# Attention, sampling and two recurrences on one core: q and k turned by transposing transfers instead of by TensorE, one-hot matrices by one comparison

## The chip, the cores and the metric

The kernel runs on one core of one Trainium2 chip. The metric is device time in microseconds of one execution, given as the median of several. Times inside an execution come from one profiled execution.

## The reference

The input x is (64, 64, 512), a condition is (64, 512). Four conditioned layers are each added to x:

```
x = x + attention(x, cond[:, None, :], W_emb, b_emb, g_norm, W_qkv, g_q, g_k, W_out)
x = x + sampling(x, cond)            # linear interpolation along the 64 tokens' features
x = x + gru_scan(cond, x, W_ih, W_hh, b_ih, b_hh)
x = x + rk4_scan(cond, cond, x, coupling, bias)
```

In attention, x is normalised by its root mean square, scaled and shifted by a modulation of the condition, and multiplied by W_qkv. Then, with 16 heads of 32:

```
q = _rms_norm(q, g_q)                # over the 32 features of a head
k = _rms_norm(k, g_k)
logits = jnp.einsum('bhqd,bhkd->bhqk', q, k) * d ** (-0.5)
attn = jax.nn.softmax(logits, axis=-1)
o = jnp.einsum('bhqk,bhkd->bhqd', attn, v)
return o + o @ W_out                 # after moving heads back
```

Sampling takes, for each batch row, the two features at floor and floor + 1 of a position given by the condition, and weighs them. The last two layers are scans over the 64 steps.

## The kernel before, in words

Two batch rows of 64 tokens make a pair of 128 tokens, which fill the partitions; there are 32 pairs, N0 being the last of them, N1 the one before. The first function, `attention_and_sampling`, works through 32 slots, one for each pair i; each engine has its own list of instructions for a slot, written out by hand, and waits on semaphores. In slot i TensorE projects pair i (`project`, three times 12 matmuls: q, k, v), computes the scores of pair i-1, mixes and projects out pair i-2, and samples pair i-3. All numbers of a matmul are f32 split into two f16 halves, high and low, and a product takes three matmuls (TERMS).

For q and k of a pair, in order: ScalarE squares the projections out of PSUM (`squares_qk`), VectorE sums them (`sums_qk`, `means`), ScalarE makes a guess of the reciprocal root by Ln and Exp (`guess`), VectorE corrects it (`newton`, three small instructions) and scales q and k by it (`scale_qk`) into the f32 tile qn. In the next slot TensorE turns qn (`turn_qk`, 8 transposes of 128x128 f32 into psA), ScalarE takes the high halves of what it turned (`high_qk`), with the gains g_q and g_k folded into q's by a scale for each partition, and VectorE the low halves (`low_qk`), both into qkT, which lies in the tile `first4` (`first` in the rows). Then `scores` runs. After scores, ScalarE computes exponentials (`exps`, 16 instructions of 128x64, one for each head, of which 2 stand ahead of the guess and 14 behind it), VectorE inverts the sums, GpSimd normalises (`norm_p`) and takes low halves (`low_halves`), and SP turns P's halves by two transposing transfers (`turn_p`, PT). The high half of V (`high_v`) stands on ScalarE behind the exponentials.

Sampling is a matmul with one-hot matrices E (in `room`). `load_rows` broadcasts the integer positions of one batch row to all partitions (`rows`, 128x512 f16), and `build` compares them with lidx, the index of a feature in its chunk, one comparison for each of 4 chunks. `weigh_taps` multiplies the samples by the interpolation weights, out of the PSUM banks that the projections of q and k use as well. So a projection waits for it:

```
            if n == 0:
                need(pe, qn_done, p.n * 2 - 1)
                need(pe, um_done, p.n * 2 - 7)
```

GpSimd modulates x of the next pair (`modulate`, two instructions), adds taps, and takes low halves of x. In slots 4 to 27 a piece of the recurrences' weights is loaded and split as well (`load_wr`, `high_wr`, `low_wr`). Before slot 0 come the condition's embedding (`high_we`, `low_we`, `embed`), the positions (`grid_front`, which waits for the condition, `condtok`), and the splitting of W_qkv. All loads but one stand in SP's queue.

The second function, `recurrences`, runs the 64 steps of both scans from about 610 us on; the change does not touch it.

## Time and profile before

| | |
|---|---|
| median of 3 runs | 1525.3 us (1524.68 to 1526.01) |
| profiled execution | 1528.0 us |
| its span | 1526.2 us |
| TensorE matmuls | 1472.8 us busy, 97% |
| VectorE | 1322.9 us, 87% |
| ScalarE | 902.6 us, 59% |
| GpSimd | 756.9 us, 50% |
| granted TensorE clock | 0.995 over the span |
| DMA | mean 55 GB/s; 100 to 130 GB/s up to about 600 us |

Busy time is the time in which an engine had an instruction at work. A busy TensorE in a stretch without idle brackets in its timeline sets the length of that stretch; another engine at a high share may still stand in a chain whose waits are what counts. In a timeline a bracket at the end of a row is the time in which the engine stood idle ahead of it and what ended that.

### The profile page before, as it was taken

How to read it: one execution, taken by the hardware profiler on the slowest of the kernel's cores; microseconds unless marked ns; L12 is line 12 of the kernel's file. 1: busy time of each engine (PE TensorE's matmuls, PEld its weight loads, DVE VectorE, ACT ScalarE, POOL GpSimd, SP SyncE). 2: the span in 40 equal slices, each digit the busy share in tenths (PEclk: the TensorE clock that was granted, in tenths of full speed). 3: DMA queues.
4: the chain of work that ended last, by engine and by line, in shares of the span. 5: the costliest groups of instructions: out<-in, count | busy, mean ns of one | idle time of the engine just before them, and what ended most of it. 6: DMA issues, size and time to landing. Idle time of an engine off the chain costs nothing.

```text
span 1526.2 us, 95000 instructions
## 1 busy us (share of the span) xinstructions
PE 1472.8 (97%) x42214; PEld 1308.4 (86%) x42214; DVE 1322.9 (87%) x3190; ACT 902.6 (59%) x2753; POOL 756.9 (50%) x916
## 2 busy tenths in 40 slices
PE   4799999999999999999999999999999999999997
PEld 2466677666776668999999999999999999999996
DVE  5888989988889878688888888888888888888887
ACT  5566776667766653555555555555555555555553
POOL 2567666666666754534434443443444344344432
PEclk9999999999999999999999999999999999999999
DMA  7255444545455432000000000000000000000000
GB/s 255 52 114 115 108 106 104 116 118 120 127 118 130 96 102 87 8 15 12 15 15 15 12 16 15 12 15 15 15 12 15 15 12 15 15 15 12 15 15 14
DMA packets 122602, 84.03 MB, mean 55 GB/s; under 512 B 68656, under 2 KB 107824, under 8 KB 122192
## 3 DMA queue, kind: packets, MB, share of 16 engines
q1 hardware_dynamic: 121968, 77.87, 20.3%
q8 instruction: 331, 5.42, 1.5%
q14 instruction: 79, 0.65, 0.2%
q10 hardware_dynamic: 224, 0.09, 0.0%
HBM read 42.23 MB, written 11.60 MB: 35 GB/s over the span
## 4 chain that ended last, share of the span: by engine, by line
PE 91%; DVE 4%; issue 2%; POOL 1%; ACT 1%; DMA 1%; SPq 0%; DVEq 0%; ACTq 0%; POOLq 0%
PE psB L1432 34%; PE psA L1461 15%; PE psQ L1146 15%; PE psA L1466 8%; PE psQ L1188 7%; PE psO L1234 5%; PE psO L1222 2%; PE psB L1170 2%; PE psA L1124 2%; DMA front<-in_cond 1%; POOL S L434 0%; DVE psO L1645 0%; POOL front L453 0%; DVE room L880 0%; PE psQ L1202 0%
## 5 line engine op out<-in xcount | busy, mean ns | idle before, releaser
L1432 PE MATMUL psB<-first,Wx 128*128 128x64 f16 x9216 | 290.3, 193 | 1.4 <-issue 1.1
L1432 PE MATMUL psB<-first,Whh 128*128 128x64 f16 x9072 | 287.0, 193 | 1.3 <-POOL first L1897 0.5
L1461 PE MATMUL psA<-ts,Cp 128*128 128x64 f16 x8160 | 280.7, 193 | 6.0 <-ACT ts L1532 6.0
L1432 PEld LDWEIGHTS psB<-first,Wx 128*128 128x128 f16 x9216 | 277.9, 98 | 2.0 <-issue 1.7
L1432 PEld LDWEIGHTS psB<-first,Whh 128*128 128x128 f16 x9072 | 274.1, 98 | 2.3 <-issue 1.4
L1146 PE MATMUL psQ<-Wx,front 128*128 128x512 f16 x1152 | 269.0, 384 | 4.1 <-DVE front L952 4.0
L1461 PEld LDWEIGHTS psA<-ts,Cp 128*128 128x128 f16 x8160 | 256.2, 98 | 7.0 <-ACT ts L1532 6.8
L1532 ACT ACTIVATE ts<-qst 128x256 f16<-128x256 f32 x192 | 80.1, 417 | 297.9 <-DVE qst L1645 297.9
L1146 PEld LDWEIGHTS psQ<-Wx,front 128*128 128x128 f16 x1152 | 108.9, 99 | 124.5 <-issue 5.0
L1897 POOL TENSOR_TENSOR en<-rz,dn 128x256 f32<-128x256 f32 x64 | 46.7, 730 | 259.8 <-issue 257.1
L1466 PE MATMUL psA<-ts,Cp 128*128 128x64 f16 x4080 | 161.2, 193 | 0.3 <-issue 0.3
L1672 DVE TENSOR_TENSOR ts<-psA,ts 128x256 f16<-128x256 f32 x255 | 107.3, 421 | 47.4 <-ACT psA L1532 47.4
L776 DVE TENSOR_SCALAR room<-rows,lidx 128x512 f16<-128x512 f16 x256 | 145.9, 612 | 0.3
L1466 PEld LDWEIGHTS psA<-ts,Cp 128*128 128x128 f16 x4080 | 136.9, 98 | 0.6 <-issue 0.4
L434 POOL TENSOR_TENSOR S<-S,rden 128x512 f32<-128x512 f32 x64 | 67.0, 1049 | 141.8 <-DVE rden L844 141.8
L518 ACT ACTIVATE S<-psB,mn 128x64 f32<-128x64 f32 x448 | 133.2, 338 | 0.0
L1645 DVE SCALAR_TENSOR_TENSOR rest<-cub,psQ 128x256 f32<-128x256 f32 x256 | 106.6, 416 | 7.3
L1645 DVE SCALAR_TENSOR_TENSOR psO<-qst,psO 128x256 f32<-128x256 f32 x253 | 107.2, 424 | 2.1
L1188 PE MATMUL psQ<-x,room 128*128 128x128 f16 x1856 | 108.5, 219 | 0.0
L1188 PEld LDWEIGHTS psQ<-x,room 128*128 128x128 f16 x1856 | 104.9, 98 | 0.1
L1897 POOL TENSOR_TENSOR V<-X3b,first 128x256 f32<-128x256 f32 x64 | 46.9, 733 | 115.9 <-DVE first L1759 114.6
L518 ACT ACTIVATION_READ_ACCUMULATOR S<-psB,mn 128x1 f32 x448 | 104.2, 233 | 0.0
(194 smaller groups left out, 2890.4 us busy)
## 6 DMA issues: line engine op xcount, KB each, us to landing
front<-in_x SPq DMA_DIRECT2D x32, 256.0 KB, 3.1
XR<-in_x_turned SPq DMA_DIRECT2D x32, 256.0 KB, 3.4
rows<-rows_dram SPq DMA_DIRECT2D x64, 128.0 KB, 3.0
out<-ob SPq DMA_DIRECT2D x63, 128.0 KB, 1.7
x<-x SPq DMA_DIRECT2D x29, 224.0 KB
Whh<-in_W_qkv SPq DMA_DIRECT2D x12, 256.0 KB, 8.4
room<-in_W_hh SPq DMA_DIRECT2D x12, 256.0 KB, 2.7
room<-in_W_ih SPq DMA_DIRECT2D x12, 256.0 KB, 3.0
```

The costliest lines, as they stand in the source:

```text
L518: return nc.scalar.activation(out, in_, f, **k)
L776: e = v.tensor_scalar(E_of(p, b)[:, k, :], rows[b][:, :], lidx[:, k:k + 1], None, ALU.is_equal)
L1146: last = mm(psQ[:, n, :], xn[p.u][:, i, c, :], Wqkv[:, j, c, n * D:(n + 1) * D], start=(c == 0 and t == 0), stop=(c == KC - 1 and t == 2))
L1188: last = mm(o[:, m, :, :], E_of(p, b)[:, c, m * PART:(m + 1) * PART], x1_of(p)[:, :, i, c, b, :], start=(c == 0 and i == 0), stop=(c == KC ...
L1234: last = mm(psO[:, m, :], Wo[:, i, c, m * PART:(m + 1) * PART], oT[:, j, c, :], start=(c == 0 and t == 0), stop=(c == KC - 1 and t == 2))
L1432: last = mm(o, W_[:, i, c, g * PART:(g + 1) * PART], src[:, j, c, :], start=False, stop=False, skip_group_check=True)
L1461: mm(psF[:, s % 2, m, :], Cp[:, i, c, m * PART:(m + 1) * PART], ts_[:, 0, c, :], start=(c == 0 and m == 0 and i == 0), stop=False, skip_gr ...
L1466: last = mm(psF[:, s % 2, m, :], Cp[:, 0, c, m * PART:(m + 1) * PART], ts_[:, 1, c, :], start=False, stop=(c == KC - 1), skip_group_check= ...
L1532: return nc.scalar.activation(out, in_, f, **k)
L1645: return v.scalar_tensor_tensor(out=flat(out), in0=flat(in0), scalar=scalar, in1=flat(in1), op0=ALU.mult, op1=op1)
L1672: v.tensor_tensor(ts_[:, 1, :, :], th, ts_[:, 0, :, :], ALU.subtract).then_inc(S["ts_ready"], 1)
L1897: return nc.gpsimd.tensor_tensor(flat(out), flat(in0), flat(in1), op)
```

## The change

For all pairs but the last, q and k are scaled into PSUM (psA), q is multiplied there by a row of gains, and both are split into f16 halves in the layout in which tokens are partitions; the halves (`qkh`, in the tile qn) are turned into qkT by two transposing transfers on SP's queue in the pair's own slot. TensorE turns only the last pair. `exps` is split into 2, 6 and 8, with the high halves of q and k between the six and the eight. The positions are stored four times, with 0, 128, 256 and 384 taken off, so that `rows` is 128x2048 and `build` is one comparison. The gains are loaded by broadcast (128x1024 f32) on ScalarE's queue, and so is the condition, which left SP's queue.

```
...
+        def turn_qk(p, n):
+            sp.wait_ge(qk_low, p.n * 2 + n + 1)
+            need(sp, sc_done, p.n)
+            sp.dma_start_transpose(qkT[:, n, :, :, :].rearrange("p i c n -> p (i c) n"), qkh[:, n, :, :].rearrange("p i n -> p (i n)"))\
+                .then_inc(qk_in, 16)
...
+            if i < NP - 1:
+                turn_qk(pair(0), 0)
+                turn_qk(pair(0), 1)
             if p := pair(-2):
                 load_rows(p, 1)
...
-                sp.dma_start(condtok, cond).then_inc(cond_in, 16)
...
         act.dma_start(vT[:, :], vectors).then_inc(vectors_in, 16)
+        act.dma_start(gains2.rearrange("p v n -> p (v n)"), gains.rearrange("v n -> (v n)").partition_broadcast(PART)).then_inc(vectors_in, 16)
+        act.dma_start(condtok, cond).then_inc(vectors_in, 16)
...
         def high_qk(p, n):
+            act.wait_ge(qn_done if n else q_gained, p.n * 2 + 2 if n else p.n + 1)
+            need(act, qk_in, p.n * 32)
+            a(qkh[:, n, 0, :], psA[:, n, :]).then_inc(qk_hi, 1)
...
-            if p := pair(-1):
-                if p.n > 1:
-                    exps(p, 2, HEADS)
-                    high_halves(p, 0)
-                else:
-                    exps_at_once(p)
+            p = pair(-1)
+            if p and p.n > 1:
+                exps(p, 2, HEADS // 2)
+            high_qk(pair(0), 0)
+            high_qk(pair(0), 1)
+            if p and p.n > 1:
+                exps(p, HEADS // 2, HEADS)
+                high_halves(p, 0)
+            elif p:
+                exps_at_once(p)
...
         def low_qk(p, n):
             dve.wait_ge(qk_hi, p.n * 2 + n + 1)
+            v.tensor_tensor(qkh[:, n, 1, :], psA[:, n, :], qkh[:, n, 0, :], ALU.subtract).then_inc(qk_low, 1)
...
-            for k in chunks:
-                e = v.tensor_scalar(E_of(p, b)[:, k, :], rows[b][:, :], lidx[:, k:k + 1], None, ALU.is_equal)
-            if chunks[-1] == KC - 1:
-                e.then_inc(e_built, 1)
+            v.tensor_scalar(E_of(p, b).rearrange("p c n -> p (c n)"), rows[b][:, :, :].rearrange("p c n -> p (c n)"),
+                            lidx[:, 0:1], None, ALU.is_equal).then_inc(e_built, 1)
...
         def scale_qk(p):
             dve.wait_ge(rs_step, (p.n + 3) * STEPS)
-            need(dve, qk_T, p.n)
+            to = sq if p.n == NP - 1 else psA
...
+                if n == 0 and p.n < NP - 1:
+                    dve.wait_ge(qn_done, p.n * 2 + 1)
+                    v.tensor_tensor(psA[:, 0, :], psA[:, 0, :], gain_row[:, :], ALU.mult).then_inc(q_gained, 1)
...
         def scores(p):
-            pe.wait_ge(qk_ready, p.n + 1)
+            if p.n == NP - 1:
+                pe.wait_ge(qk_ready, 1)
+            else:
+                pe.wait_ge(qk_in, 32 * (p.n + 1))
...
         def slot(pair, i):
-            if p := pair(-1):
-                turn_qk(p)
             project(pair(0), 0)
```

Where instructions stand now shows best in one steady slot. VectorE before, from the means of pair i on to the scaling of x for a later pair (ms are the means, rt and rs the Newton step, room the one-hot matrix, um the weighed samples, Whh a piece of weights):

```order
L785 TENSOR_SCALAR ms<-ss 128x33
L776 TENSOR_SCALAR room<-rows,lidx 128x512 x2
L865 TENSOR_TENSOR oT<-psO,oT 128x512
L790 TENSOR_TENSOR rt<-rs 128x33
L792 SCALAR_TENSOR_TENSOR rt<-rt,ms 128x33
L794 SCALAR_TENSOR_TENSOR rs<-rt,rs 128x33
L805 TENSOR_TENSOR qn<-psQ,rs 128x512 x2
L844 RECIPROCAL rden<-den 128x8
L776 TENSOR_SCALAR room<-rows,lidx 128x512 x2
...
L870 SCALAR_TENSOR_TENSOR XR<-psO,XR 128x4x128
L811 TENSOR_TENSOR Vt<-psQ,Vt 128x512
L847 TENSOR_TENSOR um<-psQ,WT 128x512
```

VectorE in the changed kernel, the same stretch:

```order
L804 TENSOR_SCALAR ms<-ss 128x33
L887 TENSOR_TENSOR oT<-psO,oT 128x512
L809 TENSOR_TENSOR rt<-rs 128x33
...
L813 SCALAR_TENSOR_TENSOR rs<-rt,rs 128x33
L824 TENSOR_TENSOR psA<-psQ,rs 128x512
L829 TENSOR_TENSOR psA<-psA,gain_row 128x512
L824 TENSOR_TENSOR psA<-psQ,rs 128x512
...
L796 TENSOR_SCALAR room<-rows,lidx 128x2048
L766 TENSOR_TENSOR qn<-psA,qn 128x512 x2
...
L892 SCALAR_TENSOR_TENSOR XR<-psO,XR 128x4x128
L833 TENSOR_TENSOR Vt<-psQ,Vt 128x512
L869 TENSOR_TENSOR um<-psQ,WT 128x512
```

Two comparisons left the place ahead of the Newton step, a multiplication by the gains stands between the two scalings, and the low halves of q and k (L766) stand ahead of V's low half, not in the next slot.

ScalarE before, from the squares of k on (front<-psQ; S are the exponentials, Vt the high half of V):

```order
L518 ACTIVATE front<-psQ 128x512
L518 ACTIVATE S,den<-psB,mn 128x64 x2
L518 ACTIVATE oT<-psO 128x512
L518 ACTIVATE lm<-ms 128x33
L518 ACTIVATE rs<-lm 128x33
L518 ACTIVATE S,den<-psB,mn 128x64 x14
L518 ACTIVATE front<-S 128x512
L518 ACTIVATE Vt<-psQ 128x512
```

ScalarE in the changed kernel:

```order
L530 ACTIVATE front<-psQ 128x512
L530 ACTIVATE S,den<-psB,mn 128x64 x2
L530 ACTIVATE oT<-psO 128x512
L530 ACTIVATE lm<-ms 128x33
L530 ACTIVATE rs<-lm 128x33
L530 ACTIVATE S,den<-psB,mn 128x64 x6
L530 ACTIVATE qn<-psA 128x512 x2
L530 ACTIVATE S,den<-psB,mn 128x64 x8
L530 ACTIVATE front<-S 128x512
L530 ACTIVATE Vt<-psQ 128x512
```

The high halves of q and k (qn<-psA) moved from the head of the next slot into the middle of the fourteen exponentials, ahead of V's.

## Rows read from the trace of the kernel before

**Rows 1.** The page, busy times and one costly group (busy, mean ns, idle):

```profile
PE 1472.8 (97%) x42214; PEld 1308.4 (86%) x42214; DVE 1322.9 (87%) x3190; ACT 902.6 (59%) x2753; POOL 756.9 (50%) x916
...
L776 DVE TENSOR_SCALAR room<-rows,lidx 128x512 f16<-128x512 f16 x256 | 145.9, 612 | 0.3
```

**Rows 2.** Timeline of TensorE in one slot: start us, us, instruction

```profile
283.52 1.04 PE L1124 MATMUL psA<-ident,qn 128*128 128x128 f32 x8
284.39 2.75 PE L1146 MATMUL psQ<-Wx,front 128*128 128x512 f16 x12
287.08 1.13 PE L1170 MATMUL psB<-first 32*64 32x64 f16 x96
...
290.83 1.20 PE L1222 MATMUL psO<-PT,Vt 64*32 64x64 f16 x96
```

**Rows 3.** Timeline of TensorE, the turns 27 slots apart

```profile
92.66 1.04 PE L1124 MATMUL psA<-ident,qn 128*128 128x128 f32 x8
...
561.02 1.04 PE L1124 MATMUL psA<-ident,qn 128*128 128x128 f32 x8
```

**Rows 4.** Timeline of ScalarE in the same slot

```profile
290.94 0.60 ACT L518 ACTIVATE front<-psQ 128x512 f32<-128x512 f32 x1 [2.12 <-PE psQ L1146]
...
293.23 0.23 ACT L518 ACTIVATE rs<-lm 128x33 f32<-128x33 f32 x1
293.36 0.30 ACT L518 ACTIVATE S<-psB,mn 128x64 f32<-128x64 f32 x1
...
297.42 0.71 ACT L518 ACTIVATE front<-S 128x512 f16<-128x512 f32 x1
297.94 0.67 ACT L518 ACTIVATE Vt<-psQ 128x512 f16<-128x512 f32 x1
```

**Rows 5.** Timeline of VectorE in the same slot

```profile
284.63 0.67 DVE L760 TENSOR_TENSOR front<-XR,psB 128x512 f32<-128x512 f32 x1
...
291.57 0.69 DVE L798 TENSOR_REDUCE ss<-front 128x16 f32<-128x512 f32 x1 [0.56 <-ACT front L518]
292.36 0.57 DVE L785 TENSOR_SCALAR ms<-ss 128x33 f32<-128x33 f32 x1
...
293.97 0.18 DVE L790 TENSOR_TENSOR rt<-rs 128x33 f32<-128x33 f32 x1
...
294.64 1.29 DVE L805 TENSOR_TENSOR qn<-psQ,rs 128x512 f32<-128x512 f32 x2
...
298.64 0.69 DVE L811 TENSOR_TENSOR Vt<-psQ,Vt 128x512 f16<-128x512 f32 x1 [0.25 <-ACT Vt L518]
299.25 0.68 DVE L847 TENSOR_TENSOR um<-psQ,WT 128x512 f32<-128x512 f32 x1
```

**Rows 6.** Line 315, P's transposing transfers: issue ns min/median/max, landing

```profile
L315 SPq DMA_TRANSPOSE PT<-front x60: 1231/1284/2365, 57.6 to 561.4; - x60
...
DMA to landing us min/median/max: 3.0/3.2/5.2
```

**Rows 7.** DMA issues: count, KB each, median us to landing

```profile
rows<-rows_dram SPq DMA_DIRECT2D x64, 128.0 KB, 3.0
...
Cp<-in_W_emb SPq DMA_DIRECT2D x2, 512.0 KB, 4.6
```

**Rows 8.** The chain that ended last, and ScalarE's timeline, at the start

```profile
4.53 8.27 DMA front<-in_cond
...
13.26 0.63 ACT L518 ACTIVATE Wx<-Whh 128x512 f16<-128x512 f32 x1 [2.00 <-DMA Whh<-in_W_qkv]
18.98 0.20 ACT L518 ACTIVATE lm<-ms 128x1 f32<-128x1 f32 x1 [5.08 <-DVE ms L785]
```

**Rows 9.** Timeline of TensorE, scores of pair 0

```profile
43.42 0.97 PE L1170 MATMUL psB<-first 32*64 32x64 f16 x96 [0.89 <-DVE first L754]
```

**Rows 10.** Timeline of GpSimd in the steady slot, its last before a pause

```profile
291.73 1.15 POOL L460 TENSOR_TENSOR front<-front 128x512 f16<-128x512 f32 x1
```

**Rows 11.** Timeline of VectorE, a Newton step beside GpSimd's work

```profile
36.31 0.34 DVE L790 TENSOR_TENSOR rt<-rs 128x33 f32<-128x33 f32 x1 [1.56 <-ACT rs L518]
```

More of the change, by code:

```diff
@@ L60, in need, with program @@
     eng.wait_ge(sem, value)
-def program(nc, x, x_turned, cond, cond_turned, vectors, W_emb, W_qkv, W_out, W_ih, W_hh, coupling_turned, out, rows_dram, wih_dram):
+def program(nc, x, x_turned, cond, cond_turned, vectors, gains, W_emb, W_qkv, W_out, W_ih, W_hh, coupling_turned, out, rows_dram, wih_dram):
     B, T, D = x.shape
@@ L160, in attention_and_sampling @@
     x1 = sb("x1", [PART, 2, 2, KC, 2, T], F16)
-    rows = [sb(f"rows{u}", [PART, D], F16) for u in range(2)]
+    rows = [sb(f"rows{u}", [PART, KC, D], F16) for u in range(2)]
     um = [sb(f"um{u}", [PART, KC, 2, T]) for u in range(2)]
@@ L917, in grid_rows @@
             dve.wait_ge(grid_step, 8)
-            v.tensor_copy(i0h, i0).then_inc(rows_ready, 1)
+            for c in range(KC):
+                last = v.tensor_scalar(i0h[:, c, :], i0, 1.0, float(-c * PART), ALU.mult, ALU.add)
+            last.then_inc(rows_ready, 1)
         def grid_weight():
@@ L976, in slot @@
                 grid_middle()
-            if tap and tap.n > 0:
-                build(tap, 0, (0,))
-            if p := pair(-1):
-                low_qk(p, 0)
-                low_qk(p, 1)
             if tap:
-                build(tap, 0, (1, 2, 3) if tap.n > 0 else range(KC))
+                build(tap, 0)
             if i == 1:
@@ L1999 @@
         vectors=np.concatenate(vectors, axis=0).T,
+        gains=np.stack([np.tile(inputs[n], D // inputs[n].shape[0]) for n in ("L0_cond_g_q", "L0_cond_g_k")]),
         W_emb=inputs["L0_cond_W_emb"], W_qkv=inputs["L0_cond_W_qkv"], W_out=inputs["L0_cond_W_out"],
```

121 lines of the change are left out of this document (59 added, 62 removed).

## The prediction

> **What bounds the kernel now.** I read first the page's busy times: TensorE works 1472.8 us of the span [rows 1], so it is the bound on average, but an average does not say where. The timeline of TensorE in one steady slot [rows 2] says it for the attention stage, which is all that the change touches: the turn of q and k (8 transposes, L1124) starts at 283.52, the first projection at 284.39, scores at 287.08, the second projection ends and mixing starts at 290.83, with no bracket of idle time anywhere. From turn to turn, over 27 slots, it is (561.02 - 92.66) / 27 = 17.35 us [rows 3], so the next turn is due at 283.52 + 17.35 = 300.87 and the next projection at 301.74. The turn takes 284.39 - 283.52 = 0.87 us of it. So TensorE is full, and an edit that takes work from it gains what the next-longest cycle allows. That cycle runs through ScalarE and VectorE, and I followed it in their timelines [rows 4, 5]: from the end of the second projection at 290.83 to the end of the first weighing of taps, 299.25 + 0.69 = 299.94, which is what the next slot's first projection waits for (`um_done`, same PSUM bank). Before, that is 1.8 us before that projection: slack.
>
> **What is taken away.** 31 of the 32 turns by TensorE go: 31 x 0.87 = 27 us of TensorE. If nothing else held it, a slot would be 17.35 - 0.87 = 16.48 us.
>
> **What is added on the cycle.** I walk the slot of [rows 2, 4, 5] with the new order of instructions.
> 1. Squares end at 290.94 + 0.60 = 291.54, the sums at 291.57 + 0.69 = 292.26, the means at 292.36 + 0.57 = 292.93, the Exp of the guess at 293.23 + 0.23 = 293.46. Unchanged.
> 2. VectorE's Newton step started at 293.97, behind two comparisons; they are gone from there, so it can start at 293.49 and ends 0.67 later (293.97 to 294.64, where the scaling starts) at 294.16.
> 3. Scaling of q 0.69 (two take 1.29, one 0.04 more than half), 294.85. Then the new multiplication by the gains, PSUM to PSUM, 128x512 f32. No row shows it; the nearest are the scalings at 0.65 each [rows 5]. Bounds: 0.65 and, if a PSUM destination costs as much again, 1.29. I take 0.69 and its hop: 295.57. Scaling of k starts one pitch (0.61) after the gain's start and ends at 296.17.
> 4. ScalarE meanwhile has done six of the fourteen exponentials: 14 take 297.42 - 293.36 = 4.06, 0.29 each, so it is free at 293.36 + 1.74 = 295.10 and waits for q until 295.60. The high halves of q and k cost like the squares out of PSUM, 0.60, with a pitch of 0.50: k's starts when its scaling is done, 296.20, and the remaining eight exponentials start at 296.70 and are over at 299.02. Before, all fourteen were over at 297.42: 1.60 later.
> 5. High half of P 0.52 (297.42 to 297.94), high half of V 0.67: 300.21. Low half of V starts behind it (before: 298.64, 0.03 behind), weighing one pitch of 0.61 later (298.64 to 299.25) and 0.69 long: 301.54. TensorE's projection can start at about 301.57.
>
> So from the end of the second projection to the next first projection it is 301.57 - 290.83 = 10.74 us, and from there over the first projection and scores to the end of the second is 290.83 - 284.39 = 6.44: a cycle of 17.18 us. TensorE itself would be ready after 16.48, so it now stands for 0.70 us in front of the first projection of each slot. **The gain is 17.35 - 17.18 = 0.17 us a slot, x 27 = 4.6 us**, not 0.87 x 27 = 23.5.
>
> **What lies beside it.** The low halves of q and k on VectorE fall into its wait for the exponentials; the one comparison over 128x2048 in front of them replaces four of 128x512, which are on no path that I found. No row shows it: it costs something above nothing and at most what four do, 4 x 0.612 = 2.4 us [rows 1]; I take 0.7. The turn itself is now a transfer: low half of k ready at 296.3 + 0.7 + 2 x 0.65 = 298.3 (1.7 later at the dear end), two issues of 1.28 each, the second from about 299.1, landing 3.2 behind its issue [rows 6]: 302.3. Scores come 2.70 after the projection's start, at 304.26: hidden by 1.9 us, by 0.2 at the dear end of the comparison. If that cover goes, each us late is a us of slot. On SP's queue behind them stand the load of the second row of indices (now 512 KB instead of 128 KB) and P's two transposing transfers. The 128 KB load lands in 3.0, a 512 KB one in 4.6 [rows 7], so I price the larger one at +1.6 us; it is wanted a slot later. P's transfers are issued about 2 us later than before, because P is, and would land about 1 us before mixing wants them.
>
> Here a rule of the Trainium skill bears on the transfer. DMA: Bandwidth & Descriptors, Latency and other measured facts, gives a transposing transfer an effective 261 GB/s; by it 256 KB is an estimated 1.0 us of transport, and the two would still be hidden. The rows show 3.2 from issue to landing and decide.
>
> **The start.** The longest single piece of the chain at the beginning is the load of the condition, issued at 4.53 and 8.27 long, and VectorE's low halves of W_emb queue behind what waits for it, so that the first guess (ScalarE, 18.98) waits 5.08 us [rows 8]. The change issues this load early from ScalarE's queue. The guess is then held by the first piece of W_qkv, whose load ScalarE waited for until 13.26 [rows 8]. The new 512 KB of gains goes in front of it, about 2 us, so 15.3, and the activation (0.63): 15.9 to 16.1 instead of 18.98. I take 2.7 us off the start; bounds 0 (the gains cost what the condition gave) and 5.
>
> **The first slots and the end.** In slots 1 and 2 the exponentials come behind the high halves of q and k, and pair 0's scores, at 43.42 before [rows 9], now wait for transfers that I place at 45.3: 1.9 later; the 0.87 no longer spent at the next turn gives part back. I take +1 us, bounds -1 and +3. At the end the turn of the last pair but one is gone as well: -0.9.
>
> **Sum.** -4.6 - 2.7 + 1.0 - 0.9 = -7.2 us against the profiled execution's own 1528.0 (span 1526.2 and 1.8 around it), which is 2.7 above the median of the runs shown: 1520.8 there, **1518 us** as a median.
>
> **The rivals.**
> - *TensorE stays the bound.* If the cycle is 0.7 us shorter than I worked out (the exponentials or halves overlap better), a slot is 16.5: -0.87 x 27 = -23.5, with the rest -26: 1499 to 1502. For it speaks that every added duration is a neighbour's; against it that the order of ScalarE's queue forces 1.6 us in. Chance 0.15.
> - *GpSimd gets in the way (ends slower).* VectorE's multiplication by 1/rms for the next pair, after which GpSimd starts, ended at 284.63 + 0.67 = 285.30, 5.5 us ahead of 290.83; now it stands behind the later weighing and ends about 4.6 ahead of it, and 3.8 where a weight's low half comes between. GpSimd's last work before its pause ended at 291.73 + 1.15 = 292.88 [rows 10]; it would end at 293.8 to 294.6, across the Newton step (293.49 on). When the two ran together at the start, the first instruction of that step took 0.34 [rows 11] against 0.18 [rows 5], so the step 1.2 against 0.67; the means would stretch too. With 0.47 more the cycle is 17.65, 0.30 longer than before: +8.1, with the rest +5.5: 1531. It decides from 0.17 on, where the gain per slot is gone. Chance 0.24.
> - *Late transfers.* If the q/k or P transfers queue behind the 512 KB loads, with landings like the longest seen, 5.2 [rows 6], scores or mixing wait. At 0.5 us a slot over mine it is +9, with the rest about 1531 to 1534. For it: two more transposing transfers and 768 KB more a slot; against: 1.9 us of cover. Chance 0.09.
> - *It cancels* within the start and slots: 1523 to 1528. Chance 0.12.
>
> On the second, the Trainium skill, GPSIMD Engine Reference, Specifications, says that GpSimd shares its SBUF interfaces with VectorE, with contention for instructions with two SBUF inputs or in a two-port mode. By that rule, the trace agrees: 0.34 against 0.18.
>
> **Numbers.** My forecast has 0.40, its own range 1511 to 1524 (cycle 16.95 to 17.35). The range over all, 1500 to 1533, leaves out part of the first and of the third rival and the far end of the second. Faster by over 0.2% (3 us, about what a measurement of this kernel can tell from no change): 0.40 + 0.15, and a little of the others: 0.58. Within: 0.15. Slower: 0.27.
>
> **What would show it.** Right: slots of 17.2 us, a bracket of about 0.7 us in front of L1162's first projection released by VectorE's weighing; ScalarE's fourteen exponentials split six and eight with k's half at about 5.4 us after the second projection; transposing q/k transfers landing over 1 us before scores; the first guess near 16.2 instead of 18.98. Wrong: no idle time before the projection (first rival); Newton instructions at 0.3 us or more (second); brackets in front of scores or mixing released by a DMA (third).

## The result and the profile after

The changed kernel takes **1547.1 us** (median of 4 runs, 1545.2 to 1548.7) against 1525.7 us of the kernel before on the same chip: a ratio of 1.0138, 95% interval 1.0121 to 1.0154. It is 1.4% slower; I had forecast it 0.5% faster. The profiled execution has a span of 1543.3 us, 17.1 more than that of before; the medians lie 21.4 apart, and the profiles locate the 17.1. One of the eight executions of e11 (below) took 3677 us, like no other, and its ratio leaves it out.

The first question is in which stage. The view by windows gives both kernels, cut at the same events (first projection, projection of slot 4, projection of slot 31, start of the recurrences); columns are the stretch and its length, busy time of the five engines with instruction counts, granted clock, DMA share, GB/s. The kernel before:

```profile
0.00:24.51 24.51, 5.81 (x98) 5.37 (x98) 11.82 (x24) 11.68 (x20) 0.86 (x9) 0.98 0.92 294
24.51:93.53 69.02, 55.90 (x825) 32.63 (x826) 56.84 (x100) 39.15 (x103) 37.84 (x36) 0.93 0.40 95
93.53:561.90 468.37, 464.17 (x9424) 333.10 (x9422) 418.19 (x758) 317.54 (x1264) 319.24 (x325) 1.00 0.48 111
561.90:612.30 50.40, 45.70 (x1200) 38.92 (x1198) 39.30 (x78) 18.20 (x32) 22.76 (x33) 1.00 0.38 110
612.30:1526.20 913.90, 901.23 (x30672) 898.44 (x30672) 796.80 (x2235) 516.02 (x1335) 376.21 (x514) 1.00 0.05 14
```

The changed kernel:

```profile
0.00:20.97 20.97, 5.43 (x97) 4.75 (x98) 12.41 (x25) 11.89 (x20) 0.86 (x9) 0.93 0.95 320
20.97:96.50 75.53, 58.22 (x794) 30.84 (x795) 60.30 (x100) 41.33 (x107) 39.23 (x36) 0.84 0.58 141
96.50:578.70 482.20, 448.07 (x9209) 310.84 (x9207) 352.90 (x624) 319.31 (x1262) 341.68 (x325) 1.00 0.77 181
578.70:627.70 49.00, 45.29 (x1198) 38.71 (x1199) 31.84 (x52) 16.91 (x30) 26.35 (x35) 1.00 0.60 177
627.70:1543.30 915.60, 900.84 (x30672) 897.38 (x30672) 796.60 (x2235) 515.89 (x1335) 376.23 (x514) 1.00 0.05 14
```

| stage | before | after | difference |
|---|---|---|---|
| to the first projection | 24.5 | 21.0 | -3.5 |
| slots 0 to 3 | 69.0 | 75.5 | +6.5 |
| 27 slots | 468.4 (17.35 each) | 482.2 (17.86 each) | +13.8 |
| end of the attention | 50.4 | 49.0 | -1.4 |
| recurrences (not touched) | 913.9 | 915.6 | +1.7 |

The page answers to [rows 1] and [rows 7] with TensorE's busy time and the rows' load:

```profile
PE 1457.9 (94%) x41966; PEld 1282.5 (83%) x41966; DVE 1254.1 (81%) x3033; ACT 905.3 (59%) x2753; POOL 784.3 (51%) x916
...
rows<-rows_dram SPq DMA_DIRECT2D x64, 512.0 KB, 5.2
```

In the 27 slots TensorE has 16 us less to do (464.2 to 448.1), so it works 99% of the time before and 93% after: it no longer sets the length of a slot. The DMA share goes from 0.48 to 0.77, which no line of the prediction looked at as a whole.

What TensorE waits for is in the view of waits of the changed kernel, 90 to 560 us (engine, what is held <- by what: us in total, times, longest; PEld is the weight load, PE the matmul behind it, so the two see the same wait and are not to be added):

```profile
PEld psQ L1162 <- issue: 24.4, 31, 1.3
PEld psO L1241 <- DMA PT<-front: 18.9, 17, 2.3
PE psQ L1162 <- DVE um L869: 18.3, 24, 1.1
PE psO L1241 <- DMA PT<-front: 10.6, 11, 1.8
```

Two waits share the slot. ("Issue" is time for which the profile shows no releaser; most of it on the first projection's weight load stands beside the matmul's wait for L869.) The first projection waits for the weighing of taps (L869) in 24 of 27 slots, as forecast; the weight loads of mixing (L1241) wait for P's transposing transfers in 17 slots and its matmuls in 11, which was forecast not to happen. One slot of the changed kernel, its timelines, start and length. TensorE, with the first projections of two slots:

```profile
293.68 2.75 PE L1162 MATMUL psQ<-Wx,front 128*128 128x512 f16 x12 [0.43 <-DVE um L869]
...
299.96 1.20 PE L1241 MATMUL psO<-PT,Vt 64*32 64x64 f16 x96
...
311.36 2.75 PE L1162 MATMUL psQ<-Wx,front 128*128 128x512 f16 x12 [1.14 <-DVE um L869]
```

VectorE:

```profile
301.49 0.76 DVE L804 TENSOR_SCALAR ms<-ss 128x33 f32<-128x33 f32 x1
...
302.81 0.56 DVE L809 TENSOR_TENSOR rt<-rs 128x33 f32<-128x33 f32 x1
...
304.60 0.70 DVE L829 TENSOR_TENSOR psA<-psA,gain_row 128x512 f32<-128x512 f32 x1
...
305.91 0.70 DVE L796 TENSOR_SCALAR room<-rows,lidx 128x2048 f16<-128x2048 f16 x1
```

GpSimd and ScalarE:

```profile
301.05 1.16 POOL L459 TENSOR_TENSOR x<-XR,x 128x512 f16<-128x512 f32 x1
302.16 1.16 POOL L472 TENSOR_TENSOR front<-front 128x512 f16<-128x512 f32 x1
305.33 1.19 ACT L530 ACTIVATE qn<-psA 128x512 f16<-128x512 f32 x2 [0.79 <-DVE psA L829]
```

SyncE's DMA queue:

```profile
307.24 2.64 SPq L325 DMA_TRANSPOSE first<-qn x2
309.93 0.57 SPq L291 DMA_DIRECT2D rows<-rows_dram x1
311.39 2.80 SPq L319 DMA_TRANSPOSE PT<-front x2
```

Read them against [rows 2, 4, 5]. From the start of mixing (299.96; 290.83 before) to the first projection it is 11.40 us, forecast 10.74. The new operations cost what was assumed: multiplication by the gains 0.70 (assumed 0.69), comparison over 128x2048 0.70 (0.7). But GpSimd's last two subtractions now end at 303.32, across the means and the Newton step, and these take 0.76 and 0.56 where [rows 5] have 0.57 and 0.18, together 0.57 of the 0.66 us (the rest is mostly a longer hop from the weighing to the projection). No wait for P's transfers stands in this slot, and it lasts 311.36 - 293.68 = 17.68 us.

How they are stretched can be read from the ends. GpSimd's subtractions end at 302.21 and 303.32, the means at 302.25 and the first Newton instruction at 303.37. The same holds throughout: between 90 and 560 us every one of the 26 means and of the 18 Newton instructions that took over 0.25 us ends 0.03 to 0.06 us behind the end of a GpSimd instruction. So they were held until it was over, not slowed by a factor. The kernel before has this too: all 26 of its long means end in that way, the 0.57 of [rows 5] among them (292.93, behind 292.88 of [rows 10]).

On SyncE's queue the second rows' load goes out 1.5 us ahead of P's transfers; before it went out 2.8 us ahead, with a quarter of the bytes. Line 319 (P), landing behind issue, minimum, median and maximum; [rows 6] had 3.0/3.2/5.2:

```profile
DMA to landing us min/median/max: 3.1/4.7/6.4
```

### The profile page after: what moved, and what is told of

Read it like the earlier page. It is cut to its first block, busy times and chain, and to the rows that moved or that the text cites. A ratio compares the mean times of both kernels' runs of the same rounds, so it can differ in the third digit from the quotient of the medians.

```text
span 1543.3 us, 94377 instructions
## 1 busy us (share of the span) xinstructions
PE 1457.9 (94%) x41966; PEld 1282.5 (83%) x41966; DVE 1254.1 (81%) x3033; ACT 905.3 (59%) x2753; POOL 784.3 (51%) x916
## 4 chain that ended last, share of the span: by engine, by line
PE 68%; DVE 11%; ACT 7%; DMA 5%; issue 5%; POOL 4%; SPq 0%; DVEq 0%; ACTq 0%; POOLq 0%
PE psB L1448 34%; PE psA L1477 15%; PE psA L1482 7%; PE psQ L1162 7%; DMA PT<-front 4%; ACT S L530 4%; DVE psA L824 3%; POOL front L452 2%; ACT front L530 1%; PE psB L1189 1%; DVE oT L887 1%; POOL S L446 1%; PE psQ L1207 1%; PE psO L1241 1%; PE psO L1253 1%
## 5 line engine op out<-in xcount | busy, mean ns | idle before, releaser
L1162 PE MATMUL psQ<-Wx,front 128*128 128x512 f16 x1152 | 275.7, 392 | 24.4 <-DVE um L869 19.7
L446 POOL TENSOR_TENSOR S<-S,rden 128x512 f32<-128x512 f32 x64 | 78.1, 1223 | 160.6 <-DVE rden L866 160.6
L817 DVE TENSOR_REDUCE ss<-front 128x16 f32<-128x512 f32 x64 | 43.8, 685 | 86.3 <-ACT front L530 86.3
L530 ACT ACTIVATE front<-psQ 128x512 f32<-128x512 f32 x64 | 38.1, 596 | 119.7 <-PE psQ L1162 119.7
```

The lines of the kernel that those rows point to most:

```text
L446: nc.gpsimd.tensor_tensor(part, part, rden[:, 8 * h:8 * h + 8].unsqueeze(2).broadcast_to([PART, HEADS // 2, T]), ALU.mult)\
L530: return nc.scalar.activation(out, in_, f, **k)
L1162: last = mm(psQ[:, n, :], xn[p.u][:, i, c, :], Wqkv[:, j, c, n * D:(n + 1) * D], start=(c == 0 and t == 0), stop=(c == KC - 1 and t == 2))
```

## The experiments

Ratios are to the kernel before on the same chip, in brackets the 95% interval. The runs were on several chips, on which the kernel before took 1523.8 to 1529.1 us (medians), so two runs are compared by their ratios: 0.001 is 1.5 us. For the steady slots I read the distance of the first and last of 27 turns of rs (one a slot, 26 distances): 17.86 us in the changed kernel, 17.35 before. Edits are to the changed kernel where nothing else is said; "..." marks what is left out of them.

### The parts one by one

**e1_narrow**: 128 KB rows and four comparisons a batch again.

```
-rows = [sb(f"rows{u}", [PART, KC, D], F16) for u in range(2)]
+rows = [sb(f"rows{u}", [PART, D], F16) for u in range(2)]
...
+            for k in range(KC):
+                e = v.tensor_scalar(E_of(p, b)[:, k, :], rows[b][:, :], lidx[:, k:k + 1], None, ALU.is_equal)
...
```

> The changed kernel with 128 KB loads of the positions and four comparisons of 128x512 again, q and k still turned by transfers. Theory (two causes in a slot: the ScalarE/VectorE cycle that ends in the weighing of taps, and P's transposing transfers held up behind the 512 KB loads): P's transfers land in about 3.2 us again instead of 4.7, TensorE's waits for them, some 15 us in all, go; the waits for the weighing stay at 0.9 a slot. About 1537 us. Rival (the transposing transfers of q and k alone hold up P's): landing stays above 4, time within 3 us of 1547.

Measured 1542.0 us, 1.0095 (1.0072 to 1.0119). Slots 17.82 us; rows land after 3.7 us, P after 4.0; TensorE's weight loads still wait 21.1 us for P's transfers, the first projections 13.2 us for the taps. By the ratios 7 us are won, but narrow rows alone don't mend the slot. The first Newton instruction is free of GpSimd in most slots here (median 185 ns), while four comparisons stand again ahead of the low halves: one delay went and another came.

**e2_wide_only**: the kernel before with the wide rows and the wide comparison, turns on TensorE.

```
-            for k in chunks:
-                e = v.tensor_scalar(E_of(p, b)[:, k, :], rows[b][:, :], lidx[:, k:k + 1], None, ALU.is_equal)
+            if chunks[0] == 0:
+                v.tensor_scalar(E_of(p, b).rearrange("p c n -> p (c n)"), rows[b][:, :, :].rearrange("p c n -> p (c n)"),
+                                lidx[:, 0:1], None, ALU.is_equal).then_inc(e_built, 1)
...
```

> The kernel before with the other part of the change alone: positions four times in a row of 128x2048, 512 KB loads, one comparison. TensorE is full in its slots there and P's halves are issued about 1 us earlier relative to mixing, so by the theory the slots stay at 17.35 and the time at 1525 to 1528, with P's landing up by 1 to 1.5 us. Rival (the wide loads or comparison are what costs the 21 us): above 1535.

Measured 1542.4 us, 1.0099 (1.0069 to 1.0128), slots 17.72 us: the part that I had costed at nothing is 15 us slower by itself. **e6_wide_loads** parts load and comparison: before with the 512 KB loads and four comparisons over 128x512.

```
...
-                e = v.tensor_scalar(E_of(p, b)[:, k, :], rows[b][:, :], lidx[:, k:k + 1], None, ALU.is_equal)
+                e = v.tensor_scalar(E_of(p, b)[:, k, :], rows[b][:, k, :], lidx[:, k:k + 1], None, ALU.is_equal)
...
```

> The kernel before with the row of numbers stored four times and loaded at 512 KB a batch, but with four comparisons over 128x512 as before. Tells the load from the comparison in the run of the wide part alone, which was 14 us slower than the kernel before although its single comparison is cheaper. Theory: the 512 KB loads cost it: two slots of about 20.3 us in which TensorE stood 1.7 to 2.1 us inside the mix of V, at an instruction that waits for no semaphore, while the DMA engines were busy for 0.8 to 1.0 of the time. Then this kernel also has such slots and takes 1535 to 1545 us. Rival: the 128x2048 comparison costs it (0.74 us at a stretch, during which another engine is held up); then this kernel takes 1525 to 1530 us.

Measured 1533.3 us, 1.0023 (1.0006 to 1.0041), slots 17.30 us. The profiled recurrences start at 615.9 us; before at 612.3, with the comparison wide as well at 621.0. So the loads cost 1 to 6 us by the interval and the rest comes with the comparison or its new places in VectorE's order. (e2, e6 and the changed kernel also set `dynamic_dma_scratch_size` to 2048, which no run tries alone.) The mechanism stays open. In e2 twelve of 26 slots still last 17.25 to 17.3 us, others up to 18.2, and two 20.3 and 20.6, in which TensorE stands 1.2 and 1.7 us inside the mix of V at an instruction that waits for no semaphore and runs its next projection at a lower clock (4.45 and 3.94 us). What differs beside it: one comparison gives the rows' buffer back sooner, and the second rows' load goes out 5.4 us ahead of P's transfers (median) in place of 2.8 in e6 and before. Whether this earlier load is the cause was not tried.

**e3_cond_early**: the kernel before with only cond's load moved to the head of ScalarE's queue.

```
+        act.dma_start(condtok, cond).then_inc(cond_in, 16)
         act.dma_start(vT[:, :], vectors).then_inc(vectors_in, 16)
...
-                sp.dma_start(condtok, cond).then_inc(cond_in, 16)
```

> The kernel before with only the load of the condition moved to the head of ScalarE's queue. If the gain of the start lasts, the first projection is at about 20.5 instead of 24.5 and the time 3 to 4 us under before, 1522. Rival (the first slots are bound by something else and give it back, as they did in the changed kernel): within 1 us of before.

Measured 1520.4 us, 0.9950 (0.9932 to 0.9968): first projection at 19.9 us, recurrences at 605.4. This one line is the only part that was faster when run by itself, and it needs nothing of the rest.

### The steady slots

**e8_small_pool**: less on GpSimd ahead of the Newton step. Its two subtractions (low halves of x1 and of the normed x) are done on one of four pieces, so three quarters of these low halves are missing in most pairs.

```
+            cs = slice(0, 1 if p.n > 4 else KC)
+            nc.gpsimd.tensor_tensor(xn[p.u][:, 1, cs, :], xa[:, cs, :, :].rearrange("p c b t -> p c (b t)"), xn[p.u][:, 0, cs, :],
...
```

> The changed kernel with GpSimd's two subtractions ahead of the Newton step (the low half of x1 and the low half of the normed x) done on one of four pieces only, about 0.3 us each in place of 1.16 us; the output then lacks three quarters of these low halves in most pairs. Theory: VectorE's means and Newton's step (0.76 and 0.56 us in the slot read) fall back to 0.57 and 0.18 us, and everything behind them on VectorE comes 0.5 us earlier, so TensorE's wait for the turned taps (19.7 us in 26 slots) nearly goes; P's transfers gain only the 0.2 us of the means. Expected 1538 to 1542 us, with the wait for P's transfers as large as before. Rival: the contention is not what sets the cycle, and the time stays within 2 us of 1547 us.

Measured 1540.3 us, 1.0084 (1.0061 to 1.0107), slots 17.47 us. The first instruction of the Newton step in 90 to 560 us, minimum, median and maximum in ns: the kernel before, the changed one, and this one:

```profile
L790 DVE TENSOR_TENSOR rt<-rs x27: 177/180/186, 103.7 to 553.9; 128x33 f32<-128x33 f32 x26, 128x32 f32<-128x32 f32 x1
```

```profile
L809 DVE TENSOR_TENSOR rt<-rs x26: 183/506/566, 105.3 to 553.2; 128x33 f32<-128x33 f32 x26
```

```profile
L811 DVE TENSOR_TENSOR rt<-rs x26: 183/185/297, 106.7 to 544.3; 128x33 f32<-128x33 f32 x26
```

The medians of the means go 395, 722, 374 ns likewise. So VectorE's small instructions lose 0.65 us a slot more than before to GpSimd working beside them, and taking that away gives 7 to 8 us of 17.6 (0.65 x 27); TensorE still waits 8.7 us for P and 10.1 for the taps. Free of GpSimd the means take 0.18 us (median of e18 below, shortest of before), so 0.2 of the kernel before's 0.395 was such a wait already.

**e4_v_first** puts v's high half ahead of q's and k's on ScalarE, and on VectorE the residual and v's low half ahead of the inversion of the second sums (still behind q's and k's low halves), so that the taps are weighed earlier; **e5_v_first_narrow** has the narrow rows too.

```
                 exps(p, 2, HEADS // 2)
+                high_v(pair(0))
             high_qk(pair(0), 0)
...
```

> The changed kernel with the high half of V ahead of the high halves of q and k on ScalarE (in its wait of 0.8 us), and on VectorE the residual and the low half of V ahead of the inversion of the second sums. The weighing of taps then no longer waits behind eight exponentials. Theory: TensorE's waits in front of the first projection, 20 us in all, go. If nothing stands behind them, slots of 16.6 and 1515 us. But P's transfers, whose chain does not get shorter, land about 17.7 to 18.3 after the second projection, and by that the slots stay at 17.7 and the time at 1540 to 1547, with the waits in front of mixing instead. I expect the second.

> The changed kernel with both v's halves ahead of q's and k's (as in the run that took TensorE's wait for the turned taps away and lengthened its wait for P's transfers) and the broadcast rows back at 128 KB with four comparisons a batch. Theory: P's transfers are late because the rows of 512 KB lie in the same DMA engines; with rows of 128 KB they land about 1 us earlier, both waits shrink together, and the 27 slots come to about 17.2 us each: 1532 us. Rival: the transfers of q and k alone fill the engines enough, P's transfers stay late, and the time is that of the two single edits, 1541 to 1550 us. Third: what stretches a slot is TensorE's clock falling after a wait of over 1 us; then the slots without such a fall are near 16.6 us and those with one near 20 us, whatever the mean is.

Measured 1551.5 us, 1.0149 (1.0117 to 1.0182), and 1559.7 us, 1.0208 (1.0193 to 1.0224). The wait for the taps goes (e5: 6.7 us left), that for P grows (weight loads 38.8 and 30.8 us). e5 shows what a longer wait costs further. TensorE in one of its slots:

```profile
210.12 2.76 PE L1167 MATMUL psQ<-Wx,front 128*128 128x512 f16 x12
214.47 1.20 PE L1246 MATMUL psO<-PT,Vt 64*32 64x64 f16 x96 [1.59 <-DMA PT<-front]
215.60 4.42 PE L1167 MATMUL psQ<-Wx,front 128*128 128x512 f16 x12
```

and the windows around it (granted clock third from the right):

```profile
196.00:206.00 10.00, 9.90 (x221) 8.33 (x221) 9.67 (x21) 8.59 (x40) 3.99 (x5) 1.00 0.44 128
206.00:216.00 10.00, 7.99 (x220) 4.09 (x219) 9.89 (x12) 4.54 (x12) 9.77 (x11) 0.98 0.84 153
216.00:226.00 10.00, 10.00 (x122) 7.59 (x121) 9.09 (x19) 8.05 (x38) 3.80 (x4) 0.85 0.63 106
```

Behind a wait of 1.6 us the same twelve matmuls take 4.42 in place of 2.76 us, with the granted clock down from 1.00 to 0.85: part of that stretch is at 1.2 of 2.4 GHz. Nine of 26 slots of e5 last 20.0 to 20.8 us, the shortest 16.4. Each of the nine has a wait for P of 1.4 to 1.8 us and such a slow projection, 4.05 to 4.45 us. The third theory of its expectation holds for the shape, but the waits come first and this is a surcharge of 1.3 to 1.7 us each time. Not every such wait brings it: the changed kernel waits 1.72 us for P at 175.72, and its next projection takes 2.76. The changed kernel has one slot with it, e4 seven.

**e9_p_first** has 11 in place of 8 exponentials ahead of q's and k's halves, **e10_rows_first** the second rows' load ahead of their transfers on SyncE, **e11_rows_p_first** both.

```
-                exps(p, 2, HEADS // 2)
+                exps(p, 2, 11)
...
-                exps(p, HEADS // 2, HEADS)
+                exps(p, 11, HEADS)
```

```
+            if p := pair(-2):
+                load_rows(p, 1)
             if i < NP - 1:
                 turn_qk(pair(0), 0)
                 turn_qk(pair(0), 1)
-            if p := pair(-2):
-                load_rows(p, 1)
```

> The changed kernel with three more of P's exponentials (11 in place of 8) ahead of q's and k's halves on ScalarE. In the slot read ScalarE waited 0.79 us for q's product with the gains, so these three (0.87 us) cost q's and k's halves about 0.1 us, and P's halves end 0.8 us earlier. q's and k's transfers have over 2 us to spare in a steady slot. Theory: P's transfers are the last to come, so TensorE's waits for them (29.5 us in all) fall by about half, and with them the slots with a lower clock: 1538 us. Rival: what makes P late is the landing time (4.7 us in place of 3.2 us) and the queue order on SyncE, and with k's half later TensorE waits longer for the turned taps: 1545 to 1550 us.

> The changed kernel with the load of the second batch's rows put ahead of the transfers of q and k in SyncE's queue, so that 512 KB no longer go out right before P's two transfers. Theory (the collision is of rows and P): P's landing falls from 4.7 to about 3.5 us, TensorE's waits for P's transfers (29.5 us in all) by more than half, q's and k's transfers land about 1.5 us later, for which a steady slot has room: 1538 us. Rival (any transfer in these 5 us holds up the others, and the sum is what counts): what P gains q and k lose, waits for them appear at the scores, and the time stays within 2 us of 1547 us.

> The same with 11 in place of 8 exponentials ahead of q's and k's halves. That edit alone took TensorE's wait for the turned taps away (0.5 us left of 18.3 us) but P's landing rose from 4.7 to 5.7 us, as its transfers went out 2.5 us earlier and into the rows' load. Theory: with the rows out of the way both gains hold, the slots come to 16.6 to 17.0 us, and the time to 1530 us. Rival: P lands when q's, k's and its own transfers have gone through, whatever the order; then as with the rows moved alone, or 1545 us.

| | us | ratio | slot | P lands after | waits for taps (PE) | for P (PE) | for q, k (PE) |
|---|---|---|---|---|---|---|---|
| changed kernel | 1547.1 | 1.0138 | 17.86 | 4.7 | 18.3 | 10.6 | 0 |
| e9 | 1546.0 | 1.0120 (1.0096 to 1.0145) | 17.73 | 5.7 | 0.5 | 24.1 | 0 |
| e10 | 1545.9 | 1.0129 (1.0109 to 1.0149) | 17.77 | - | 21.7 | under 1 | 5.0 |
| e11 | 1533.8 | 1.0037 (1.0017 to 1.0057) | 17.28 | 3.3 | 0.7 | 3.0 | 11.2 |

Each edit alone removes one of the two waits, another takes its place, and 1 to 3 us are won, less than the width of the intervals. In e9 the lower clock takes back part of the gain: five of its slots have the slow projection, and the projections of 26 slots take 7 us more than in the changed kernel (223.4 and 216.7). Together the two edits win 15 us by the ratios (13 by the medians). The waits of e11, 90 to 560 us:

```profile
PEld psB L1189 <- DMA first<-qn: 20.1, 19, 2.5
PE psB L1189 <- DMA first<-qn: 11.2, 11, 2.0
PEld psO L1241 <- DMA PT<-front: 8.5, 12, 1.2
PE psQ L1162 <- DVE um L869: 0.7, 3, 0.3
```

The landing shows that order on the queue matters: in e9 P's transfers went out about 1 us earlier (median 10.3 us behind the start of mixing in place of 11.2; the 2.5 us of e11's expectation is wrong) and 0.7 us behind the rows' load in place of 1.4, and landed 1 us later behind their issue (5.7); in e11, with the rows out of the way, after 3.3. Now q's and k's transfers land late, after 4.7 in place of 2.8 us, as they follow the rows.

**e7_no_k**: k is not turned by a transfer from the third pair on, so the scores use an old k.

```
+            if n == 1 and p.n > 1:
+                sp.dma_start(qkT[0:1, n, 0, 0, 0:16], qkh[0:1, n, 0, 0:16]).then_inc(qk_in, 16)
+                return
```

> The changed kernel with only q turned by a transposing transfer; from the third pair on k's halves are not moved (a few bytes go in its place, so the scores use an old k). Theory: the two transfers of q and k stand ahead of the second batch's rows in SyncE's queue and push these rows to within 1.5 us of P's transfers, which then land after 4.7 us in place of 3.2 us; with one of the two gone, rows and P come 1.3 us earlier, P's landing falls to 4 us or less and the waits for P's transfers by at least half: 1536 to 1540 us. Rival: P is late by its exponentials, which stand behind q's and k's halves on ScalarE (unchanged here): the waits for P and the time stay, 1545 us.

Measured 1544.0 us, 1.0110 (1.0095 to 1.0125). P lands after 3.8 us and matmuls wait 1.1 us for it; but the wait for the taps is 25.7 us and the slot 17.68. The theory of the queue is right on the landing and wrong on the time, as the other wait stood ready.

**e18_all_three**: e11 and e8 together.

> The changed kernel with the second rows' load ahead of q's and k's transfers, 11 exponentials ahead of their halves, and GpSimd's two subtractions ahead of the Newton step done on one of four pieces (the output lacks three quarters of these low halves in most pairs). If the three causes are separate and are all there is in a steady slot, their gains add (13 and 7 us from 1547 us: 1527 us) and most slots last 16.4 us, TensorE's own work. Rival: with q's and k's transfers landing after 4.7 us behind the rows, the scores wait for them as they do without the third edit (31.3 us in 27 slots), less contention only moves the halves and gains up to 3 us: 1531 to 1534 us.

Measured 1524.3 us, 0.9986 (0.9968 to 1.0004), slots 17.04 us; the shortest last 16.38. The gains add: by the ratios 15 and 8 us, and 23 measured. What is left are mainly waits of 10.3 us for q's and k's transfers. TensorE's own work is the bound of 16.4 us in some slots only. None of e9 to e18 has the narrow rows, though e1 won 7 us with them and e2 points the same way; that combination was not run.

### The first slots

**e12_fill**: 29 matmuls of 128x512, whose result nobody reads, in four waits of slots 0 to 2.

```
...
+        def fill(count):
+            for _ in range(count):
+                mm(psO[:, :, :].rearrange("p c n -> p (c n)"), Wqkv[:, 0, 0, 0:PART], Wqkv[:, 0, 0, 0:D], start=True, stop=True)
...
```

> The changed kernel with 29 matmuls of 128x512 on old operands, whose result nobody reads, in four places of slots 0 to 2 where TensorE waits (6 and 10 at the ends of slots 0 and 1, 8 ahead of the first scores, 5 ahead of the first mix). Theory: the 6.5 us that slots 0 to 3 take longer than before come with TensorE's clock (0.84 granted in place of 0.93 there), which falls because TensorE stands 3 to 4 us at these places; with work in them the clock stays and projections of 4.4 to 5.1 us fall to 2.8 us: 4 to 6 us less, 1541 to 1543 us. Rival: the matmuls only cost their own time (up to 2 us where a wait is shorter than they are), and slots 0 to 3 are set by the transfers of q and k and of P: 1547 to 1549 us.

Measured 1547.9 us, 1.0137 (1.0122 to 1.0152). The first projection of slot 2 takes 2.75 instead of 5.14 us, yet the time is the same: slots 0 to 3 together last 70.4 us in place of 71.0 from turn to turn of rs, and a wait of 2.89 us for o's halves now stands in slot 2. The clock is a symptom there. The slots, from first projection to first projection (before 24.51, 39.78, 53.53, 72.44, 93.53; changed 20.97, 34.83, 54.07, 74.88, 96.50), differ by -1.4, +5.5, +1.9 and +0.5 us, so nearly all of the 6.5 us is lost in slot 1. What holds it is on the timelines, in the changed kernel, of VectorE, SyncE, TensorE and ScalarE:

```profile
33.98 0.70 DVE L824 TENSOR_TENSOR psA<-psQ,rs 128x512 f32<-128x512 f32 x1
...
37.23 2.71 SPq L325 DMA_TRANSPOSE first<-qn x2
...
42.35 1.50 PE L1189 MATMUL psB<-first 32*64 32x64 f16 x96 [3.08 <-DMA first<-qn]
...
52.70 1.05 ACT L530 ACTIVATE S<-S 128x1024 f32<-128x1024 f32 x1
...
53.80 0.48 PE L1261 MATMUL psB<-ident,rs 128*128 128x128 f32 x1 [3.96 <-ACT S L530]
```

From the scaling of q to the scores it is 42.35 - 33.98 = 8.4 us; before, by the same two events, 37.51 (the scaling's start) to 43.42 [rows 9], 5.9. And the exponentials of pair 0, whose input was ready at 46.4 (the subtraction on VectorE starts at 45.15 and takes 1.23), start at 52.70 behind q's and k's halves of pair 1; TensorE waits 3.96 us for them.

**e14_once_first** puts these exponentials first in slots 1 and 2; **e15_three** does it in e11.

```
                 exps(p, 2, HEADS // 2)
+            elif p:
+                exps_at_once(p)
             high_qk(pair(0), 0)
...
```

> The changed kernel with the exponentials of pairs 0 and 1 (done at once) ahead of q's and k's halves on ScalarE in slots 1 and 2. Theory: in slot 1 these exponentials were ready at 46.4 us, stood behind the halves until 52.70 us, and TensorE waited 3.96 us for their end before it turned the rs of the third next pair; put first they start at about 49.4 us as before, slot 1 falls from 19.7 to about 16.5 us, slot 2 by 1 us, and the kernel to 1542 or 1543 us. Rival: q's and k's halves are 1.05 us later and the transfers of q and k set slots 1 and 2, so that less than 1.5 us is won: 1546 us.

> All three edits of order in the changed kernel: the second rows' load ahead of q's and k's transfers on SyncE, 11 exponentials ahead of their halves, and the exponentials of pairs 0 and 1 ahead of them too. The first two gave 1533.8 us together. Theory: the third adds its 4 us, as it acts in slots 1 and 2 alone: 1529 to 1530 us, as fast as before or 0.2% slower. Rival: nothing added: 1534 us.

Measured 1545.2 us, 1.0138 (1.0114 to 1.0163), and 1534.5 us, 1.0072 (1.0046 to 1.0098). In e14 slot 1 falls from 19.7 to 17.2 us (turn of rs to turn of rs), but slots 2 and 3 take 1.5 and 1 us more; the scores of slots 1 to 3 wait 5.1, 3.5 and 2.0 us for q's and k's transfers, in the changed kernel 3.1, 0 and 0.5. So the rival holds: an exponential earlier wins nothing, as these transfers take it back.

**e16_rows_apart** moves the second rows' load of e15 to the middle of the next slot.

> The same, and the load of the second batch's rows moved from right ahead of q's and k's transfers to the middle of the next slot, behind the first batch's rows. Theory: in the kernel with the two edits of order what is left of TensorE's waits is for q's and k's transfers (31.3 us over 27 slots; they land after 4.7 us, 2.8 us without a load ahead of them); with the load away they land after 2.8 us and P's after 3.3 us, these waits fall by two thirds and the slots to 16.6 us: 1521 to 1525 us, faster than before. Rival: the load now collides with the pieces of x1 and of the weights moved in the middle of the slot, the comparison waits for it, and the time stays at 1530 us or rises.

Measured 1535.6 us, 1.0078 (1.0052 to 1.0103). q's and k's transfers land after 2.8 us and the scores wait 0.6 us for them in all, but the rows land after 6.2, and the sampling waits 10.0 us for the comparison. The load only changed victims.

**e17_cond_fill**: e3 with filling matmuls (12 small ones ahead of the first projection, 15 of 128x512 in slots 0 to 2).

> The kernel before with cond's load ahead of the others on ScalarE's queue (1520.4 us), and matmuls whose result nobody reads in four waits of TensorE: 12 of 128x128 f32 ahead of the first projection, 6 and 2 of 128x512 at the ends of slots 0 and 1, 7 ahead of the scores of slot 2. Theory (a clock that falls in a wait costs what the next projection takes longer, where this projection is on the path): the first projection takes 2.75 in place of 5.03 us and those of slots 1 and 2 are 1.3 and 1.6 us shorter: 3 to 4 us less, 1517 us. Rival, as in the changed kernel: the waits behind them get longer by the same, 1520 us.

Measured 1519.5 us, 0.9970 (0.9957 to 0.9983), no better than e3 within what the intervals tell, as they overlap; e3, with one line moved, is the version to keep.

## Why the prediction was wrong

The sign was wrong. Point by point, against the profiled spans (forecast -7.2, found +17.1):

- **The bound before, and TensorE's own slot: right.** It was full; without the turn its work is 16.4 us a slot (forecast 16.48), seen in the shortest slots of e5, e11 and e18.
- **The cycle over ScalarE and VectorE: right path, a term left out.** The projection does wait for the weighing of taps, and every new instruction cost what was assumed. The step that failed is the sum "301.57 - 290.83 = 10.74 us", which took the means as in [rows 5] and the Newton step at 0.67. It came to 11.40, and 0.57 of the difference (0.65 by the medians) is VectorE's small instructions held by GpSimd: my second rival, priced at 0.47 and given 0.24. The passage even located GpSimd's end at 293.8 to 294.6, across a step that starts at 293.49; it should have been the main line. The slot read above, with nothing else in it, lasts 17.68 us against 17.18 forecast and 17.65 of that rival. By that rule of the Trainium skill (GPSIMD Engine Reference, Specifications) the trace agrees for the first Newton instruction, which has two inputs in SBUF: 506 ns against 180, and 185 with GpSimd's work cut (e8). That the whole wait for the taps, 18.3 us, comes near the forecast 0.70 x 27 = 18.9 is partly luck, as the slot read waits 1.14.
- **"P's transfers ... would land about 1 us before mixing wants them": the other step that failed, a wait put at nothing.** It rests on the landing of 3.2 us of a kernel whose DMA share is 0.48. The rows' load, four times as large, now goes out 1.5 us ahead of P's transfers, because both transfers of q and k stand in front of it on the same queue, and P lands after 4.7 us. I had listed what stands behind on the queue and priced the load (+1.6, measured 5.2 against 3.0), but priced it for itself and not for what follows it. The late-transfers rival had 0.09. Both signs of being wrong that the prediction names for these two rivals, Newton instructions of 0.3 us or more and a bracket in front of mixing released by a DMA, are there.
- **The two waits hide each other.** 27 slots were 18 us longer than forecast (17.86 against 17.18). By the slot read, the hold by GpSimd makes about 0.5 of the 0.68 us and P's lateness, with one slow projection behind it, the rest; this split is an estimate from one slot. Neither can be seen in full by curing the other: e4, e7, e9 and e10 each remove one and move the time by 4 us at most, in either direction; e11 removes two and gives 15 us, e18 three and gives 23.
- **The comparison at 0.7 us, "on no path that I found": size right, claim wrong.** e2 shows the wide form 15 us slower with no change of q and k, of which e6 puts 1 to 6 on the loads. Why is open.
- **The start: right in the number.** -3.5 (forecast -2.7, bounds 0 and -5). The cause was partly another: the guess is not held by the first piece of W_qkv, which was there at 13.74, but by VectorE's means, and comes at 15.44 in place of 15.9 to 16.1:

```profile
15.44 0.20 ACT L530 ACTIVATE lm<-ms 128x1 f32<-128x1 f32 x1 [1.07 <-DVE ms L804]
```

  In e3 the guess comes at 12.33 and the first projection only at 19.9, so the guess alone does not set it. e3 shows the earlier load to be worth 5 to 10 us for the whole (its interval).
- **The first slots: +6.5, forecast +1.0 with bounds -1 and +3.** This term was mis-sized. q's and k's way from scaling to scores is 2.5 us longer (a gain, two issues of 1.3 and a landing in place of a turn of 0.87; I had priced 1.9), and in slot 1 nothing overlaps it; the exponentials of pair 0 then start at 52.70, and TensorE waits 3.96 us for them (1.85 before), which I had named and not priced by itself. Slot 1 alone takes 5.5 us more.
- **The end:** -1.4, forecast -0.9.
- **The range** took in 1533 at its upper end, the price of each slow rival by itself; the two hold together, and with the first slots make 1547.

## What to carry to other kernels

A transfer that replaces work on the bounding engine brings its issue time and its place on the queue with it: write down the queue's new order, and for every transfer that is now late ask which one lands behind it, and price the landing for the queue's new load, not the old one. Where two waits end within a microsecond of each other, remove both in one experiment before judging either; one at a time they showed 1 to 4 us here, together 15. Look at when a small VectorE instruction starts against GpSimd's: it was held to the end of the GpSimd instruction beside it, so moving it into such an instruction costs what is left of that. And test the small parts of a large change alone: one load moved to another queue was the only one that paid.

## What the runs showed of the hardware

- The time of the recurrences, which no edit touches, varied by more than I expected: from their first matmul to the end of the span 911.7 us (e14) to 923.6 (e6), with 913.9 before. Single profiled spans of this kernel can't tell 5 us apart; the stages and the medians can.
- A wide load up to 1.5 us ahead of a transposing transfer goes with a landing 1.5 to 2.5 us later (3.2 to 4.7, and 5.7 us at 0.7 us ahead in e9); moved away, 3.3 (e11).
- TensorE's wait of 1.59 us in e5 was followed by a projection of 4.42 in place of 2.76 us, at a granted clock of 0.85; in the changed kernel one of 1.72 us was followed by a projection of 2.76. The length of the wait alone does not tell.
- A VectorE instruction of 0.18 us takes 0.51 us (median) when it starts while GpSimd subtracts, and each stretched one ends 0.03 to 0.06 us behind the end of GpSimd's instruction, in the kernel before and in the changed one. The means, 0.18 us when free (e18), take 0.40 before and 0.72 after.
